# Turning the normed rows of a second MLP with two transposing DMAs instead of TensorE

## What is computed

```
def rmsnorm(x, w):
    var = jnp.mean(jnp.square(x), axis=-1, keepdims=True)
    return x * jax.lax.rsqrt(var + EPS) * w
...
h = rmsnorm(x, postnorm_w)                # 256 features
out = x + gelu(h @ mlp_w1 + mlp_b1) @ mlp_w2 + mlp_b2
```

## Time and profile before

| | us |
|---|---|
| median of 3 runs | 1121.99 |
| lowest and highest | 1121.43, 1122.46 |
| span of the profiled execution | 1120.9 |
| TensorE busy | 1077.3 |
| VectorE busy | 973.0 |
| ScalarE busy | 960.3 |
| GpSimd busy | 560.8 |

### The profile page before, as it was taken

One profiled execution on the slowest core, in us unless ns is written; L12 is line 12 of the kernel. 1 busy time (PEld: TensorE's weight loads), 2 busy tenths in 40 slices (PEclk: granted clock), 3 DMA queues, 4 the chain that ended last, 5 costly groups with the idle time before them and its releaser, 6 DMA issues.

```text
span 1120.9 us, 46846 instructions
## 1 busy us (share of the span) xinstructions
PE 1077.3 (96%) x19624; PEld 942.0 (84%) x19624; DVE 973.0 (87%) x2360; ACT 960.3 (86%) x2155; POOL 560.8 (50%) x807
## 2 busy tenths in 40 slices
PE   6688999999999999999999999999999999999998
PEld 5677788888888888888888888888888888888887
DVE  4899988888899888889988888999888899998774
ACT  3558988998888899988888998888899888899887
POOL 3757555454544545454454445455444555554322
PEclk9999999999999999999999999999999999999999
DMA  7541000000000000000000000000000000000000
GB/s 262 185 163 40 17 19 15 9 15 19 14 13 19 20 15 18 19 14 13 19 19 20 14 18 19 8 19 19 19 15 19 19 8 20 23 8 8 7 7 21
DMA packets 30435, 34.13 MB, mean 30 GB/s; under 512 B 11920, under 2 KB 28048, under 8 KB 29200
## 3 DMA queue, kind: packets, MB, share of 16 engines
q1 hardware_dynamic: 30224, 31.14, 8.7%
HBM read 26.93 MB, written 4.19 MB: 28 GB/s over the span
## 4 chain that ended last, share of the span: by engine, by line
PE 57%; DVE 24%; ACT 7%; POOL 6%; issue 4%; DMA 1%; SPq 0%; DVEq 0%; ACTq 0%; POOLq 0%
PE psum L482 23%; PE psum L662 11%; PE psum L622 6%; PE psum L495 5%; PE psum L456 4%; PE psum L589 3%; PE psum L608 3%; DVE mx_self L1318 3%; POOL prob_self L2561 3%; DVE prob_self L1337 3%; DVE late L1301 3%; DVE prob_self L1308 2%; DVE spread_lat L1268 2%; DVE mx_ctx L1318 2%; ACT xn_mlp L1967 1%
## 5 line engine op out<-in xcount | busy, mean ns | idle before, releaser
L2561 POOL TENSOR_TENSOR prob_self<-prob_self,add_self 128x512 f32<-128x512 f32 x64 | 84.8, 1342 | 146.8 <-DVE prob_self L1308 146.7
L2561 POOL TENSOR_TENSOR prob_cross<-prob_cross,add_cross 128x512 f32<-128x512 f32 x64 | 81.0, 1286 | 88.8 <-DVE prob_cross L1308 88.8
L2040 ACT ACTIVATE staging<-psum,cols,undo_in 128x128 f32<-128x128 f32 x256 | 95.8, 456 | 2.2 <-PE psum L482 1.7
L2040 ACT ACTIVATE hid_mlp<-psum,folded,undo_in 128x128 f32<-128x128 f32 x256 | 97.0, 472 | 0.1
L662 PE MATMUL psum<-hi_m,parts_mlp 128*128 128x256 f16 x512 | 94.6, 273 | 0.9 <-DVE parts_mlp L1370 0.9
L662 PE MATMUL psum<-hi_n,staging 128*128 128x256 f16 x512 | 94.1, 273 | 1.1 <-ACT headsT_lat L1988 0.6
L482 PE MATMUL psum<-xT_mlp,hi_m 128*128 128x128 f16 x1024 | 92.6, 219 | 0.1
L482 PE MATMUL psum<-xT_mlp,hi_n 128*128 128x128 f16 x1024 | 92.5, 219 | 0.0
L2567 POOL TENSOR_TENSOR late<-late,mx_ctx 128x512 f32<-128x512 f32 x64 | 67.2, 1050 | 45.2 <-DVE mx_ctx L1324 42.1
L482 PE MATMUL psum<-xT_mlp,lo_n 128*128 128x128 f16 x512 | 89.0, 219 | 0.0
L482 PE MATMUL psum<-xT_mlp,lo_m 128*128 128x128 f16 x512 | 89.0, 219 | 0.0
(11 more groups left out here) (281 smaller groups left out, 4045.8 us busy)
## 6 DMA issues: line engine op xcount, KB each, us to landing
xin<-in_x SPq DMA_DIRECT2D x32, 128.0 KB, 2.1
ctxT<-in_ctxT SPq DMA_DIRECT2D x32, 128.0 KB, 2.0
late<-in_ctxT SPq DMA_DIRECT2D x4, 1024.0 KB, 9.0
late<-in_x SPq DMA_DIRECT2D x4, 1024.0 KB, 6.6
out<-xb SPq DMA_DIRECT2D x32, 128.0 KB, 2.1
staging<-in_w_m SPq DMA_DIRECT2D x2, 1024.0 KB, 6.6
staging<-in_w_n SPq DMA_DIRECT2D x2, 1024.0 KB, 5.4
mask<-in_mask_cross SPq DMA_DIRECT2D x32, 32.0 KB, 1.9
```

The costliest lines, as they stand in the source:

```text
L2040: last = e.activation(hid[t][g][:, j * P:(j + 1) * P], ps[:, j * P:(j + 1) * P], ACT.Gelu_apprx_tanh, bias=b1[:, 4 * g + j:4 * g + j + 1], ...
L2561: e.tensor_tensor(ch, ch, over_heads(a[:, :]), ALU.add).then_inc(sem["added_" + t], 1)
```

## The change

The normed rows of `mlp1` are split before they are turned, in the layout they have. ScalarE writes the high half in f16 (`high_pair`) into a new tile `pair_mlp1` (128 x 2 x 256), VectorE makes the low half beside it from the residual and `rstd` (`low_pair`: x * rstd - high), and SyncE turns each half with a transposing DMA straight into `x_hi["mlp1"]` and `x_lo["mlp1"]` (`turn_across`). TensorE's `turn`, and ScalarE's `high_half` of `mlp1` are gone; `hidden` waits for the two DMAs; `root` waits for `x_lo_mlp1`. `high_pair` stands where `normalize` stood, `low_pair` where `low_half` stood.

The diff, cut to one place of each kind:

```
-        xn = {t: sb("xn_" + t, [P, H]) for t in ("self", "cross", "mlp0", "mlp1")}
+        xn = {t: sb("xn_" + t, [P, H]) for t in ("self", "cross", "mlp0")}
+        pair = sb("pair_mlp1", [P, 2, H], F16)
...
             def hidden(u, t, g, b):
                 q.wait_ge("lo_mlp", {"mlp0": 1, "mlp1": 4}[t])
-                q.wait_ge("x_lo_" + t, u + 1)
+                if t == "mlp1":
+                    q.wait_ge("across_hi_mlp1", 16 * (u + 1))
+                    q.wait_ge("across_lo_mlp1", 16 * (u + 1))
+                else:
+                    q.wait_ge("x_lo_" + t, u + 1)
...
                 score(t - 2, "self", 2)
-                turn(t - 6, "mlp1", 5)
                 v_cross(t - 3, 4)
...
+            def low_pair(u):
+                q.wait_ge("x_hi_mlp1", u + 1)
+                q.wait_ge("across_lo_mlp1", 16 * u)
+                e.scalar_tensor_tensor(pair[:, 1, :], residual("mlp1", u)[:, :], rstd["mlp1"][:, 0:1], pair[:, 0, :],
+                                       ALU.mult, ALU.subtract).then_inc(sem["x_lo_mlp1"], 1)
...
                 divided(t - 5, "lat")
-                low_half(t - 6, "mlp1")
+                low_pair(t - 6)
                 largest_score(t - 2, "self", 0)
...
+            def high_pair(u):
+
+                q.wait_ge("across_hi_mlp1", 16 * u)
+                q.wait_ge("rstd_mlp1", u + 1)
+                e.activation(pair[:, 0, :], residual("mlp1", u)[:, :], ACT.Copy, scale=rstd["mlp1"][:, 0:1]).then_inc(sem["x_hi_mlp1"], 1)
...
                 high_half(t - 2, "self")
-                normalize(t - 6, "mlp1")
+                high_pair(t - 6)
...
                 exponential(t - 3, "cross", 1)
-                high_half(t - 6, "mlp1")
                 values(t - 3, "cross")
...
-                q.wait_ge("xn_" + t, u)
+                q.wait_ge("x_lo_mlp1" if t == "mlp1" else "xn_" + t, u)
...
+            def turn_across(u):
+
+                q.wait_ge("x_hi_mlp1", u + 1)
+                q.wait_ge("hid_mm_mlp1", 2 * u)
+                q.wait_ge("across_hi_mlp1", 16 * u)
+                e.dma_start_transpose(x_hi["mlp1"], pair[:, 0, :]).then_inc(sem["across_hi_mlp1"], 16)
+                q.wait_ge("x_lo_mlp1", u + 1)
+                q.wait_ge("across_lo_mlp1", 16 * u)
+                e.dma_start_transpose(x_lo["mlp1"], pair[:, 1, :]).then_inc(sem["across_lo_mlp1"], 16)
...
                 store(t - 10)
+                turn_across(t - 6)
...
             store(UNITS - 4)
+            turn_across(UNITS - 2)
+            turn_across(UNITS - 1)
             store(UNITS - 3)
```

More of the change, by code:

```diff
@@ L247, in build @@
         xb = [sb(f"xb{i}", [P, H]) for i in range(IN_FLIGHT)]
-        xn = {t: sb("xn_" + t, [P, H]) for t in ("self", "cross", "mlp0", "mlp1")}
+        xn = {t: sb("xn_" + t, [P, H]) for t in ("self", "cross", "mlp0")}
+        pair = sb("pair_mlp1", [P, 2, H], F16)
         heads = {t: sb("heads_" + t, [P, H]) for t in ("self", "cross", "lat")}
-        xT = {t: sb("xT_" + t, [P, KH, P]) for t in ("self", "cross", "mlp0", "mlp1")}
+        NORMED = ("self", "cross", "mlp0", "mlp1")
+        xT = {t: sb("xT_" + t, [P, KH, P]) for t in NORMED}
         headsT = {t: sb("headsT_" + t, [P, KH, P]) for t in ("self", "cross", "lat")}
@@ L276, in build @@
         part = {t: [a[:, :].bitcast(F16) for a in parts[t]] for t in parts}
[L277 to L282, removed]
+        bn = {t: sb("bn_" + t, [P, 6]) for t in NORMED}
+        mv = {t: sb("mv_" + t, [P, 2]) for t in NORMED}
+        var = {t: sb("var_" + t, [P, 1]) for t in NORMED}
+        rstd = {t: sb("rstd_" + t, [P, 1]) for t in NORMED}
+        minus_mean = {t: sb("minus_mean_" + t, [P, 1]) for t in NORMED}
+        shift = {t: sb("shift_" + t, [P, 1]) for t in NORMED}
         mean_square = sb("mean_square", [P, 1])
@@ L836, in _ @@
             score(2, "ctx", 6)
-            turn(0, "mlp1", 4)
             heads_turn(1, "lat", 5)
@@ L971, in _ @@
             v_self(UNITS - 1, 1)
-            turn(UNITS - 5, "mlp1", 3)
             mix(UNITS - 2, "cross", 2)
@@ L1014, in _ @@
             prob_turn(UNITS - 1, "cross", 1)
-            turn(UNITS - 4, "mlp1", 6)
             q_lat(UNITS - 2, 4)
@@ L1042, in _ @@
             v_ctx(UNITS - 1, 5)
-            turn(UNITS - 3, "mlp1", 6)
             lat_turn(UNITS - 1, 7)
@@ L1065, in _ @@
             heads_turn(UNITS - 1, "lat", 6)
-            turn(UNITS - 2, "mlp1", 7)
             project(UNITS - 1, "lat", 5)
@@ L1605, in _ @@
             largest_score(2, "lat", 0)
-            low_half(0, "mlp1")
+            low_pair(0)
             largest_score(2, "lat", 1)
@@ L1720, in _ @@
             masked(UNITS - 4, "ctx", 0)
-            low_half(UNITS - 6, "mlp1")
+            low_pair(UNITS - 6)
             masked(UNITS - 4, "ctx", 1)
@@ L1770, in _ @@
             lat_low(UNITS - 3)
-            low_half(UNITS - 5, "mlp1")
+            low_pair(UNITS - 5)
             denominators(UNITS - 2, "cross")
@@ L1827, in _ @@
             k_spread(UNITS - 2, "lat", 1)
-            low_half(UNITS - 4, "mlp1")
+            low_pair(UNITS - 4)
             add_residual(UNITS - 1, "cross")
@@ L1850, in _ @@
             q_bias_lat(UNITS - 1)
-            low_half(UNITS - 3, "mlp1")
+            low_pair(UNITS - 3)
             k_spread(UNITS - 1, "lat", 0)
@@ L1873, in _ @@
             divided(UNITS - 1, "lat")
-            low_half(UNITS - 2, "mlp1")
+            low_pair(UNITS - 2)
             add_residual(UNITS - 1, "lat")
@@ L1877, in _ @@
             hidden_lo(UNITS - 3, "mlp1", 1)
-            low_half(UNITS - 1, "mlp1")
+            low_pair(UNITS - 1)
             hidden_lo(UNITS - 2, "mlp1", 0)
@@ L2179, in _ @@
             prob_out(1, "lat", 1)
-            normalize(0, "mlp1")
+            high_pair(0)
             heads_out(1, "lat")
-            high_half(0, "mlp1")
             normalize(3, "mlp0")
@@ L2244, in _ @@
             gelu(UNITS - 7, "mlp1", 1)
-            normalize(UNITS - 6, "mlp1")
+            high_pair(UNITS - 6)
             prob_out(UNITS - 5, "lat", 1)
@@ L2290, in _ @@
             exponential(UNITS - 2, "cross", 1)
-            normalize(UNITS - 5, "mlp1")
+            high_pair(UNITS - 5)
             prob_out(UNITS - 2, "cross", 0)
@@ L2328, in _ @@
             exponential(UNITS - 1, "cross", 1)
-            normalize(UNITS - 4, "mlp1")
+            high_pair(UNITS - 4)
             lat_out(UNITS - 2)
@@ L2350, in _ @@
             prob_out(UNITS - 2, "ctx", 1)
-            normalize(UNITS - 3, "mlp1")
+            high_pair(UNITS - 3)
             prob_out(UNITS - 2, "lat", 1)
@@ L2371, in _ @@
             prob_out(UNITS - 1, "lat", 1)
-            normalize(UNITS - 2, "mlp1")
+            high_pair(UNITS - 2)
             hidden_hi(UNITS - 3, "mlp1", 0)
@@ L2375, in _ @@
             heads_out(UNITS - 1, "lat")
-            high_half(UNITS - 2, "mlp1")
             hidden_hi(UNITS - 3, "mlp1", 1)
             gelu(UNITS - 2, "mlp1", 0)
-            normalize(UNITS - 1, "mlp1")
+            high_pair(UNITS - 1)
             hidden_hi(UNITS - 2, "mlp1", 0)
-            high_half(UNITS - 1, "mlp1")
             gelu(UNITS - 2, "mlp1", 1)
```

28 lines of the change are left out of this document (13 added, 15 removed).

## The result

The changed kernel takes 1134.02 us (median of 4 runs, 1131.16 to 1135.99), the kernel before 1122.22 (4 runs, 1121.43 to 1124.42). The ratio is 1.0103, 95% interval 1.0085 to 1.0122: slower by 1.0%. The profiled execution is the shortest of the four: 1131.16 us, a span of 1129.4.

What follows compares the result with a forecast made beforehand. VectorE with GpSimd was taken to bound the part of each slot where the change acts, TensorE the rest. Span 1120.9 + 11.5 (loop) + 2.7 (ends) = 1135.1, median 1.1 above, stated as 1136.0 us; range 1123 to 1146.

Steps and rivals of the forecast that it cites:

- the ends: Units 0, 30 and 31, where the transposes are not hidden: +2.7 us in all at T = 2.5.
- The bound: Main loop, 572.87 to 584.4: VectorE's chain with GpSimd bounds, so the removed turn and cast are worth nothing there.
- The stop: VectorE and GpSimd keep each other from SBUF at low_pair: +0.46 us a slot, 11.5 us over 25 slots.
- GpSimd's second addition begins at 575.35: Step in the loop: the addition waits for low_pair's end at 575.27, ends at 576.61, making shifted 0.46 us later.
- T: Time of a transposing DMA from issue to landing, taken as 2.5 us, with 2.1 and 9.0 kept as bounds.
- Fill: Unit 0: the low half lands at 161.7 where hidden(0) started at 160.78, +0.9 us.
- Unit 31: High DMA waits for unit 30's last hidden, low one 0.33 later: +1.3 us, less 0.2 for the removed turn.
- Unit 30: low_pair follows heads_lat, its transpose lands at 1104.9 against 1104.21: +0.7 us.
- Two holders, no cost: Rival: VectorE's instruction between GpSimd's two additions costs nothing, only the ends stay: 1122 to 1125 us; chance 0.15.
- A slow transpose: Rival: from T = 9.4 on TensorE waits in each slot; T = 11 gives above 1185 us; chance 0.05.
- GpSimd goes first again: Rival: both additions run before low_pair, mx_self starts 1.5 us later each slot, about 1162 us; chance 0.04.
- Faster: Rival: TensorE's order sets the slot, 32 removed turns save 7 us, about 1118 us; chance 0.06.

Runs made afterwards that it cites:

- The port alone: Kernel before, all turns on TensorE, no transposing DMA, but mlp1's low half computed from residual and high half in SBUF: 1124.23 us, ratio 1.0017.
- the low half alone: Changed kernel with units 0, 30 and 31 turned by TensorE and only low_pair moved to where GpSimd is idle: 1121.03 us, ratio 1.0000.
- the three units' run: Changed kernel with units 0, 30 and 31 turned by TensorE as before, 1 to 29 by DMAs: 1124.38 us, ratio 1.0016.
- the swapped order: Changed kernel with SyncE's turn_across(0) put ahead of load_rest(6): 1129.19 us, ratio 1.0064.
- the repeated one: The changed kernel run once more without an edit, for a second profile: 1133.07 us, ratio 1.0097 to the kernel before.
- the masks' move: VectorE's denominators(t - 5, "lat") put behind the two masked of self; alone in the kernel before: 1121.63 us, ratio 1.0002.
- the first kernel with three units on TensorE: Changed kernel with only units 0, 30 and 31 turned by TensorE, low_pair and denominators at their old places: 1124.38 us, ratio 1.0016.

## Why the prediction was right, and where it was not

The direction and the total came true: 1136.0 was predicted, 1134.02 measured, inside 1123 to 1146. The direction rests on terms that all came with the right sign, but that the total came so near is luck: two terms missed in opposite directions. The loop was put at +11.5 and gave +2.0; the ends were put at +2.7 and gave +7.5 to 8.7. Of the signs that the prediction named for being right, `pair_mlp` came at its length and TensorE's busy share fell; the additions (2.68 us, not 2.9) and the period (32.68, not 33.1) did not come.

**The bound (right).** The removed turn and cast were taken to be worth nothing in the loop, for VectorE's chain covers them. The port alone, with the turns on TensorE, has the same 32.68 as the change without them: in this kernel they are worth nothing. Without the stop they seem to be worth something: VectorE then goes from `mx_self` to `over_cross` with no gap (575.30 + 0.60 = 575.90 with the low half alone), where the kernel before started it 0.07 us later, released by TensorE.

**The stop (right), its size (wrong).** `pair_mlp` at 0.79 us against 0.8 to 0.9 expected, `mx_self` 0.17 us later against its mask (577.58 - 575.33 = 2.25, from the earlier trace rows 574.95 - 572.87 = 2.08) against 0.24. The Trainium skill's rule ("SBUF — State Buffer", section "SBUF: two separate sides") gives a full block of the later one. For VectorE these rows agree: the same instruction takes 0.79 us beside GpSimd and 0.48 alone. For GpSimd they don't: its second addition is 0.18 us longer beside an instruction of 0.48.

The step that failed is "GpSimd's second addition begins at 575.35". It was to be pushed by the whole length of `pair_mlp`, and `shifted` by 0.46. In its row it begins where it did (2.01 us behind `masked`) and takes 1.45 us instead of 1.27; a stop stands in a row as length, as that of `pair_mlp` does. So its end comes 0.18 us later and not 0.46, and the two additions take 2.68 us, not 2.9. How the two share the time the rows don't show. `shifted` is 0.19 later at its end (578.57 + 0.77 - 575.33 = 4.01 against 575.94 + 0.75 - 572.87 = 3.82 from the earlier trace rows). So the hand-over is softer than a whole instruction each way: `pair_mlp` and the second addition together need some 0.3 us less than their lengths in a row would.

Then part of the 0.19 ran into slack that the prediction didn't look for: before, `over_cross` started 0.07 us later than VectorE's queue would have let it, released by TensorE (`mx_self` at 576.62 + 0.60 = 577.22, start 577.29). Of 0.19, 0.09 is left at `late` and 0.08 in the period. The term was 11.5 us and measured 2.0. The prediction's own lower end, 0.24 a slot or 6.0 us, was too high as well.

**T (right).** 2.5 taken, 2.3 measured. The bounds beside it were misread: 2.5 is not the slowest small transfer of the kernel before (in its DMA view `mask_self`, 16 KB, has 7.9) and 9.0 not the longest (`rows`, 640 KB, has 10.5). Nothing came of it, as T lay near the low end. The estimate of 2.6 from the Trainium skill's 1309 ns a block ("VectorE: DVE Perf Modes", section "The three transpose paths") is near it too, but not as a rule per block, by which four would be an estimated 5.2: they landed in 2.4 us.

**The ends (wrong).** 2.7 us predicted; 7.5 in the profiled execution, 8.7 by the three units' run. Three things were missing.
- Fill, +0.9: the DMAs were costed from the moment of their data, not from SyncE's place in its list. `turn_across(0)` stands behind `load_rest(6)`, which waits for GpSimd's `keys_mask` (ends 156.06) and takes SyncE to 158.2. That is 2.1 us, as the swapped order shows. "Each queue that it is moved past" had been looked at in the loop only.
- Unit 31, +1.1 net: the prediction had "the low one is issued behind it, 0.33 later by a plain issue". But a transposing issue holds SyncE 1.17 us. The wait is 2.2 us longer than before instead of 1.1 (hidden to hidden 3.77 us, against 1108.20 to 1109.73 in the earlier trace rows, 1.53). One transpose for both halves takes this back.
- The clock had no term: 1.5 us at the end of the profiled execution (17.92 us from unit 31 on, against 16.37 where it stayed full), 2.5 at the fill of the repeated one. Unit 30 (+0.75, predicted +0.7) has neither.

**The rivals.** "Two holders, no cost", 1122 to 1125, is what the loop nearly did: without the ends the change gives 1124.4. "A slow transpose", "GpSimd goes first again" and "Faster" did not occur.

## What to carry to other kernels

Place an instruction with two SBUF operands where GpSimd is idle: here that was worth 0.13 to 0.18 us a slot, where the change cost 0.08. With the three units on TensorE it brought the time back to that of before (1.0000), and only with the masks' move as well to a small gain (0.9982). A DMA on a path that nothing hides costs its place in the issuing queue, its issue and its landing, each to be read apart; keep the old way for the first and last units, where the pipeline hides nothing, and use the DMA for the rest. And a forecast whose total fits should still be read term by term: 11.5 + 2.7 = 14.2 and 2.0 + 8.7 = 10.7 lie much nearer to each other than their terms do.

## What the runs showed of the hardware

- **A wait of 2.5 to 3 us can halve TensorE's clock, and need not.** It fell to 0.50 behind waits of 3.04, 3.19, 2.83, 2.46 and twice 2.47 us, and once behind 0.76 us, before unit 30, where waits of 0.81 and 0.68 us stood shortly ahead; it did not behind 2.97 and 2.48, nor in two other runs behind 0.77 with 0.81 and 0.69 ahead of it. Where both cases are at hand the fall goes with 1.4 to 2.5 us. It has a part in the spread of the changed kernel's runs (4.8 us, 1131.16 to 1135.99), but not alone: the eleven runs of the first kernel with three units on TensorE are 1.4 us apart, while other kernels that wait for no transpose have single runs 3 to 6 us above their median, also at a lower mean clock (the kernel before: 1124.67 at 0.991, most at 0.994 to 0.997). From unit 0 to the last matmul the 13 profiles have no fall but within or right behind such waits. That the clock follows what TensorE did just before agrees with the Trainium skill ("TensorE: Matmul & The Clock Gate", section "What's actually happening"); what decides between two equal waits no run here shows.
- **A transposing DMA from SBUF to SBUF** holds SyncE 1.17 to 1.2 us at the median, up to 2.4 now and then in the loop, where plain issues have medians of 0.33 (`xin`) to 0.59 (`keys_i`), and lands after 2.3 us for 64 KB and 2.4 for 128 KB.
- **Two instructions that share the port** did not exclude each other in full: GpSimd's second addition became 0.18 us longer (1.45 against 1.27) beside a VectorE instruction of 0.48, and its start did not move.
